# Early tile table kept in PSUM, its shares made with it, and GpSimd ending at its last scatter: one RWKV and mixture-of-experts kernel on one core

## What is computed

```python
x = x + attn(layernorm(x))          # attn: LN, token shift, k, v, r, wkv scan, Wo, then relu^2 FFN with a gate
xn = layernorm(x)
scores = xn @ gate_w.T              # [4096, 8]
topk_scores, topk_idx = top_k(scores, 2)
probs = softmax(topk_scores)
h1, h2 = split(xn @ w12[e].T)       # for the two experts e of a token
y = sum(probs * ((silu(h1) * h2) @ w3[e].T))
return x + y
```

## Time and profile before

| | us |
|---|---|
| median of three executions | 330.01 |
| the profiled execution, as timed | 332.63 |
| span of the profiled execution, first to last instruction | 330.8 |
| busy: TensorE | 260.2 (79%) |
| busy: VectorE | 241.2 (73%) |
| busy: GpSimd | 212.0 (64%) |
| busy: ScalarE | 196.4 (59%) |
| mean granted TensorE clock | 0.92 |

### The profile page before, as it was taken

One profiled execution on the slowest core, in us unless ns is written; L12 is line 12 of the kernel. 1 busy time (PEld: TensorE's weight loads), 2 busy tenths in 40 slices (PEclk: granted clock), 3 DMA queues, 4 the chain that ended last, 5 costly groups with the idle time before them and its releaser, 6 DMA issues.

```text
span 330.8 us, 6269 instructions
## 1 busy us (share of the span) xinstructions
PE 260.2 (79%) x1684; PEld 206.3 (62%) x1684; DVE 241.2 (73%) x735; ACT 196.4 (59%) x412; POOL 212.0 (64%) x225
## 2 busy tenths in 40 slices
PE   0684869999979999794796899379998799999300
PEld 0231347485746758482385799279998799999200
DVE  3076799899979799799959656776666366666790
ACT  3554288798876887585387267226676467675000
POOL 5215147625786887978376676777777777766760
PEclk9997899999989999998599599879999999999855
DMA  7930000000011111111254011142522333336583
GB/s 264 425 114 0 1 0 2 32 3 33 32 65 34 33 40 42 48 39 61 58 130 106 33 54 60 43 121 67 137 82 71 93 106 96 93 95 204 197 290 129
DMA packets 22418, 29.23 MB, mean 88 GB/s; under 512 B 4317, under 2 KB 15583, under 8 KB 22128
## 3 DMA queue, kind: packets, MB, share of 16 engines
q1 hardware_dynamic: 14832, 13.45, 14.4%
q0 software_dynamic: 4352, 8.47, 7.7%
q10 hardware_dynamic: 3200, 6.90, 5.6%
HBM read 15.09 MB, written 12.14 MB: 82 GB/s over the span
## 4 chain that ended last, share of the span: by engine, by line
DVE 26%; PE 20%; POOL 14%; issue 14%; DMA 6%; SPq 2%; ACT 2%; POOLq 0%; DVEq 0%; ACTq 0%
POOL res_d L459 8%; PE p_up L839 7%; POOL rows_d L442 3%; DVE st L897 3%; PE p_up L746 2%; PE p_f L758 2%; DMA res_d<-yo,xg 2%; DVE p_up L959 2%; DMA o_raw<-res_d 2%; DVE num L952 2%; DVE full L1101 2%; DVE xm L1003 2%; DVE den L948 1%; DVE mv L904 1%; DVE early L1117 1%
## 5 line engine op out<-in xcount | busy, mean ns | idle before, releaser
L442 POOL DMA_INDIRECT rows_d<-rows,pos x64 | 65.5, 1024 | 22.4 <-issue 21.8
L839 PE MATMUL p_up<-xgT,w_up 128*128 128x128 f32 x576 | 73.2, 282 | 2.2 <-DVE hid L1131 1.8
L839 PEld LDWEIGHTS p_up<-xgT,w_up 128*128 128x128 f32 x576 | 69.8, 198 | 2.5 <-issue 2.5
L459 POOL DMA_INDIRECT res_d<-yo,xg x48 | 47.9, 997 | 17.9 <-issue 17.0
L1127 DVE SCALAR_TENSOR_TENSOR gate_h<-th,p_up 128x512 f32<-128x512 f32 x36 | 24.7, 687 | 37.4 <-ACT th L615 36.4
L635 ACT ACTIVATE w_up<-w_exp 128x512 f32 x72 | 41.3, 622 | 7.0 <-DVE slot_w L1111 4.3
L615 ACT ACTIVATE th<-p_up 128x512 f32<-128x512 f32 x36 | 21.5, 596 | 34.4 <-PE p_up L839 32.1
L746 PE MATMUL p_up<-ysum,w_sb 128*128 128x512 f32 x64 | 35.6, 656 | 2.4 <-POOL ysum L421 2.4
L758 PEld LDWEIGHTS p_f<-wfv_half,kk 128*128 128x128 f32 x256 | 30.8, 192 | 3.9 <-issue 3.3
L758 PE MATMUL p_f<-wfv_half,kk 128*128 128x128 f32 x256 | 32.2, 278 | 0.0
L704 PE MATMUL p_up<-xn,w_mix 128*128 128x512 f32 x32 | 20.1, 714 | 15.1 <-DVE rw L966 11.8
(11 more groups left out here) (167 smaller groups left out, 562.1 us busy)
## 6 DMA issues: line engine op xcount, KB each, us to landing
o_raw<-res_d SPq DMA_DIRECT2D x16, 256.0 KB, 5.5
xg<-rows_d SPq DMA_DIRECT2D x48, 65.0 KB, 1.9
w_exp<-experts ACTq DMA_DIRECT2D x1, 3072.0 KB, 16.9
x_all<-x SPq DMA_DIRECT2D x10, 256.0 KB, 2.3
out<-x_all ACTq DMA_DIRECT2D x8, 256.0 KB, 2.4
o_raw<-rows_d SPq DMA_DIRECT2D x24, 65.0 KB, 2.0
x_all<-x SPq DMA_DIRECT2D x1, 1536.0 KB, 16.7
rows_d<-rows,pos POOLq DMA_INDIRECT x64, 2.4
```

What stands on the lines that cost most here:

```text
L442: pool.indirect_dma_start(out=rows_d[:, :], out_offset=bass.IndirectOffsetOnAxis(ap=row, axis=0), in_=rows_of[c % 2][:, t, k, :], in_offse ...
L459: pool.indirect_dma_start(out=res_d[:, :], out_offset=bass.IndirectOffsetOnAxis(ap=row, axis=0), in_=yo[b][:, n, :], in_offset=None, bound ...
L839: mm = pe.matmul(p_up[b][:, n, h * P:(h + 1) * P], w_up[q % 2][:, n, h * P:(h + 1) * P], xgT[q % 2][:, n, :], start=True, stop=True)
```

## The change

The small tiles of the first table become slices of the PSUM bank `p_k`, where the counts already are. Its steps stay, in a slightly other order: the minimum with 24 is taken twice (once to `early_cum` in SBUF, once to PSUM), the reduction for the first rows comes ahead of the one for the experts. The five share steps of (8, 12) move to the end of `early_table`, one of them becoming a copy and one a tensor_tensor with a broadcast operand. `up(0)` waits for the table's eleventh step instead of its first. At the end VectorE adds all eight chunks of the first half; GpSimd has nothing behind its last scatter, and SyncE, behind its last load, waits for the scatters instead.

```diff
+EARLY_LINKS = 11
...
+            for u in range(BUFS):
+                sp.wait_ge(S[f"scattered{u}"], 32 * LATE_ROUNDS)
...
             for q in range(3, PAIRS):
                 scatter(q)
 
-            pool.wait_ge(S["x3_kept"], 16 * CHUNKS)
-            for c in range(DVE_CHUNKS, CHUNKS):
-                add_result(pool, 0, c, "lower_added_pool")
-
-            for u in range(BUFS):
-                pool.wait_ge(S[f"scattered{u}"], 32 * LATE_ROUNDS)
...
                 if q == 0:
-                    pe.wait_ge(S["early_steps"], 1)
+                    pe.wait_ge(S["early_steps"], EARLY_LINKS)
                     pe.wait_ge(S["rw_ready"], CHUNKS)
...
-                early_link(dve.tensor_scalar(part[:, :], p_k[:, 0:E], 1.0 / P, (1 - P) / (2.0 * P), ALU.mult, ALU.add))
-                early_link(dve.tensor_scalar(full[:, :], part[:, :], WHOLE, -WHOLE, ALU.add, ALU.add))
-                dve.tensor_tensor_scan(full_cum[:, :], ones_e[:, :], full[:, :], 0.0, ALU.mult, ALU.add)
-                early_link(dve.tensor_scalar(full_coef[:, :], full[:, :], -float(P), float(REGION), ALU.mult, ALU.add))
...
+                counts, part, full, full_cum, coef = (p_k[:, n * E:(n + 1) * E] for n in range(5))
+                until, shares, steps = (p_k[:, n * E:(n + 1) * E] for n in range(5, 8))
+                first, expert = p_k[:, 64:64 + some], p_k[:, 64 + some:64 + 2 * some]
+                early_link(dve.tensor_scalar(part, counts, 1.0 / P, (1 - P) / (2.0 * P), ALU.mult, ALU.add))
+                early_link(dve.tensor_scalar(full, part, WHOLE, -WHOLE, ALU.add, ALU.add))
+                dve.tensor_tensor_scan(full_cum, ones_e[:, :], full, 0.0, ALU.mult, ALU.add)
+                early_link(dve.tensor_scalar(coef, full, -float(P), float(REGION), ALU.mult, ALU.add))
+                early_link(dve.tensor_tensor(past[:, 0:some, :], spread_e(slot_no[:, 0:some], some), spread_s(full_cum, some),
+                                             ALU.is_ge))
+                dve.tensor_scalar(early_cum[:, 1:E + 1], full_cum, float(EARLY_SLOTS), None, ALU.min)
+                dve.tensor_scalar(until, full_cum, float(EARLY_SLOTS), None, ALU.min)
+                early_link(dve.tensor_tensor(past_rows[:, 0:some, :], past[:, 0:some, :], spread_s(coef, some), ALU.mult))
+                early_link(dve.tensor_reduce(first, past_rows[:, 0:some, :], mybir.AxisListType.X, ALU.add))
                 dve.scalar_tensor_tensor(out=slot_row[:, 0:some], in0=slot_no[:, 0:some], scalar=float(P),
-                                         in1=slot_first[:, 0:some], op0=ALU.mult, op1=ALU.add).then_inc(S["early_row"], 1)
+                                         in1=first, op0=ALU.mult, op1=ALU.add).then_inc(S["early_row"], 1)
+                early_link(dve.tensor_reduce(expert, past[:, 0:some, :], mybir.AxisListType.X, ALU.add))
+                dve.tensor_scalar(slot_w[:, 0:some], expert, float(E - 1), float(EW), ALU.min, ALU.mult)\
                     .then_inc(S["early_w"], 1)
-            def early_shares(_):
...
+                early_link(dve.tensor_tensor(shares, until, early_cum[:, 0:E], ALU.subtract))
+                early_link(dve.tensor_copy(early[:, 0:E], shares))
+                dve.tensor_tensor(late_base[:, :], slot_no[:, :], shares[:, 0:1].to_broadcast([P, LATE_SLOTS]), ALU.add)
+                early_link(dve.tensor_tensor(steps, early[:, 1:E + 1], shares, ALU.subtract))
+                early_link(dve.tensor_scalar(step_coef[:, :], steps, float(P), float(REGION), ALU.mult, ALU.add))
...
-                     {(8, 6): [(gate_hidden, 0)], (8, 12): [(early_shares, 0)],
-                      (9, 2): [(gate_hidden, 1), (weigh, 0)],
+                     {(8, 6): [(gate_hidden, 0)], (9, 2): [(gate_hidden, 1), (weigh, 0)],
...
-            for c in range(DVE_CHUNKS):
-                add_result(dve, 0, c, "lower_added")
...
+            for k in range(TOPK):
+                for c in range(CHUNKS):
+                    after(dve, "lower_added", k * (c + 1))
+                    add_result(dve, k, c, ("lower_added", "higher_added")[k])
```

More of the change, by code:

```diff
@@ L119, in build @@
         total_i = sb("total_i", [P, E], I32)
-        part = sb("part", [P, E]); full = sb("full", [P, E]); full_cum = sb("full_cum", [P, E])
-        full_coef = sb("full_coef", [P, E]); early_cum = sb("early_cum", [P, E + 1]); early = sb("early", [P, E + 1])
+        early_cum = sb("early_cum", [P, E + 1]); early = sb("early", [P, E + 1])
         step_coef = sb("step_coef", [P, E]); late_base = sb("late_base", [P, LATE_SLOTS])
@@ L268, in fill_pads @@
                 eng.dma_start(rows_d[bass.ds(n + e * REGION, P), :], pad[:, :]).then_inc(S["pad_filled"], 16)
-        DVE_CHUNKS = 5
         def add_result(eng, k, c, done):
@@ L1109, in early_table @@
+                early_link(dve.tensor_reduce(first, past_rows[:, 0:some, :], mybir.AxisListType.X, ALU.add))
                 dve.scalar_tensor_tensor(out=slot_row[:, 0:some], in0=slot_no[:, 0:some], scalar=float(P),
-                                         in1=slot_first[:, 0:some], op0=ALU.mult, op1=ALU.add).then_inc(S["early_row"], 1)
-                dve.tensor_scalar(slot_w[:, 0:some], slot_e[:, 0:some], float(E - 1), float(EW), ALU.min, ALU.mult)\
+                                         in1=first, op0=ALU.mult, op1=ALU.add).then_inc(S["early_row"], 1)
```

## The result

| | before | changed |
|---|---|---|
| median (range) | 330.07 us (329.98 to 332.33) | 318.02 us (317.63 to 318.60) |
| ratio, 95% interval | | 0.9621 [0.9577, 0.9664] |
| profiled execution; its span | 332.63; 330.8 | 318.60; 316.8 |

What follows compares the result with a forecast made beforehand. Bound by a chain of waits across engines, with tiny VectorE steps held by GpSimd's tensor_tensors, and at the end by GpSimd's drain. Profiled 332.63 minus 7.9 (front) minus 5.0 (end) is 319.7; less 2.62 offset, median 317.1 us, range 315.3 to 323.3.

Steps and rivals of the forecast that it cites:

- Table: First table on VectorE, moved to PSUM: `full` 0.16 instead of 5.05 us, `slot_row` some 4.8 earlier, `receptance` 3.5 earlier.
- the value 0: Hold assumed for the first table's PSUM-to-SBUF steps under GpSimd's tensor_tensors, chosen between bounds 0 and 4.9 us.
- C: Rival: the first table's steps still touch SBUF, so `full` or a later step waits to 156.8; 323.4 us; chance 0.07.
- TensorE: First table's stage: waits for `rw` and first early rows go, clock rises 3.4 us sooner; gain 2.8, bounds 1.1 and 2.8.
- Second stall: At (8, 12): shares leave, `var` is held instead, 2.6 us stay; `var` and gate_hidden(1) come 6.1 us earlier.
- The fall at 182: TensorE's clock fall at 182.2, blamed on its waits before up(2), should not come: 3.05 us, bounds 0 and 3.05.
- Front: Stages up to GpSimd's last x3: 7.9 us gained, taken between 8.8 and 7.1; 4.2 if the clock falls again.
- the upper case: Front gain of 8.8 us: GpSimd's work moves 6.0 earlier and its 2.81 wait before the last x3 goes.
- The end: After the last scatter: adds go to VectorE, GpSimd's 9.2 us drain starts at that scatter's end; 5.0 us gained.
- A: Rival at the end: drain runs its 9.2 us only after scatters land; tail gains 0.3, 321.8 us; chance 0.22.
- D: Rival at the end: loads and stores in flight stretch the drain; slower, 335.3 us at three times its length; chance 0.03.
- The sum: Whole kernel: profiled 332.63 minus 7.9 minus 5.0 gives 319.7; with the 2.62 us offset to the median, 317.1.

Runs made afterwards that it cites:

- e3: Kernel before with the first table in PSUM, but the share steps still at (8, 12) in SBUF and the old end; 324.72 us, ratio 0.9879.
- e2: Changed kernel with the old end: table in PSUM, shares made with it, GpSimd adding three chunks and waiting for its scatters; 323.32 us, ratio 0.9851.
- e4: Kernel before with the share steps moved right behind the first table, all still in SBUF, old end; 327.41 us, ratio 0.9958.
- e1: Kernel before with only the new end: VectorE does all adds, SyncE waits for the scatters; 324.64 us, ratio 0.986.

## Why the prediction was right, point by point

- **Table.** `full` 0.17 (0.16 forecast). From `full`'s start to the end of `slot_row` 1.99 us instead of 6.98, 5.0 earlier (4.8); `rw` 3.66 earlier (3.5). The steps from PSUM to SBUF that no row of before showed took 0.17: the value 0, taken by `rw`, holds, and C is out.
- **TensorE.** Of the two waits only the one for `rw` went. The forecast had the loads follow `slot_row`; the first rows now end a wait of 0.96 us, with 0.31 and none in the other two profiles. The clock rose at 159.7, 159.6 and 160.9 us instead of 165.1, 4.2 to 5.5 sooner (3.4 forecast). None of this reached the sum: the way to the last x3 is the same in all three. The 2.8 us "at TensorE" was sized for a path that no longer bounds.
- **Second stall.** `var` of chunk 6 is the next held, 0.84 us, as said; against the start of `full` it ends 6.4 us earlier (6.1). The parts hold as well. The forecast's 3.5 from the table has the shares' 1.0 us ahead of `rw` taken off; counted with the shares it is 4.5 for the table alone and 2.6 - 1.0 = 1.6 for moving the shares. Measured on GpSimd's chain: 4.7 (e3) and 1.7 (e3 to e2, and e4).
- **The fall at 182.** It is gone in all three profiles of the changed kernel, as forecast. The reason given, that it follows TensorE's waits, isn't borne out: e1 and e3 have the wait of 1.77 and 1.78 us before up(2) and no fall. What brings it stays open. GpSimd's wait for the last `ffn` goes with it in three profiles of the same code: 2.81 us where the fall lasts 6.8, 1.38 where it lasts 3.4, none where there is no fall.
- **Front.** 7.9 forecast, between a case of 7.1 and one of 8.8. Against the profiled run of before the way to the last x3 shrank by 9.2: 6.4 for GpSimd's chain (6.0 forecast) and the wait of 2.81, which is the upper case. The step down from 8.8 to 7.9 stood for a late TensorE that did not bound. Against the two other profiles with the old table and shares it shrank by 7.7 and 7.5, the same 6.4 and smaller waits.
- **The end.** 5.0 forecast, 15.95 to 10.94 measured, 5.0; drain 9.2 after the last scatter's end, and ACT 0.8 ahead of it, "within a us" (0.2 behind it in the third profile). A and D are out: with 3.5 us of scatters, the loads and the stores in flight the drain took its 9.2.
- **The sum.** The profiled run was forecast at 319.7 and was 318.60: 14.0 less instead of 12.9 (9.2 at the front, 5.0 at the end, 0.6 between them, and a start of `full` 0.9 later). The mechanism held; the step of the sum that was off most is the last one: the 2.62 us by which the profiled run of before lay above its median were carried over as they were, where that of after lies 0.58 above its own. Some 1.5 to 1.7 us of them (50.18 to 48.68 and 48.45) are the longer wait for `ffn` in that very run, whose going was counted in the 7.9 already. So 317.1 came out 0.9 low: 1.1 too little gain, 2.0 too much offset. That the two misses partly cancel is luck.

## What to carry to other kernels

Where two engines share a lock, look for the small instruction of the held form: an operand in PSUM, or another operation, frees it at no cost seen here (0.16 to 0.17 us in either form). It pays only if its consumer isn't queued behind the same row of the other engine: freeing `full` paid, freeing `var` didn't. What an engine does last decides when its closing work starts: end each engine with its last issue and leave the waiting to one whose drain is short (SyncE's took 7 ns here). And where one profile lies above the median, ask which stall in it makes the difference before taking both the offset and the stall's removal. The same holds for stages compared by single profiles: take out the waits that come and go between profiles of one program before adding up parts.

## What the runs showed of the hardware

- GpSimd's drain took 9214 ns in each of the six profiles where it had nothing queued before it, and where it was queued behind scatters it ended 9.2 to 9.4 us after the last. ACT's took 8 ns.
- The falls of TensorE's clock wander between profiles of one program, by position and by length (3.4, 6.8 or 10.2 us, 17.1 in e1 from 150.1). In the changed kernel a fall ahead of `full` stood at 135.8 us in one profile and near 115 to 116 in the other two.
- The last three scatters of the changed kernel, which run while VectorE's adds (two inputs in SBUF) follow one another, take 1.42 to 1.50 us, and 0.97 else. It isn't so each time: in e2 and in the second profile of the kernel before, the last scatter has such an add beside it and takes 0.97. The Trainium skill (SBUF — State Buffer, "Who interferes with whom") infers that a VectorE tensor_tensor takes only the read side of the shared pair and leaves the making of descriptors alone; a scatter here also reads its row numbers from SBUF, so these rows don't decide whether that inference holds. The adds themselves kept a pace of 0.61 us (9.71 for 16).
